# Second and third level of the expert mix on GpSimd: once for all five slabs of a group

## The reference, cut to what matters

```python
def _L0_ffn_ref(x, router_w, router_b, expert_w, expert_b):
    B, N, D, C, E, K = (8, 4096, 64, 64, 8, 2)
    router_probs = jax.nn.softmax(x @ router_w + router_b, axis=-1)
    top_p, top_i = jax.lax.top_k(router_probs, K)
    top_p = top_p / jnp.sum(top_p, axis=-1, keepdims=True)
    expert_out = jnp.einsum('bnd,edc->bnec', x, expert_w) + expert_b
    gathered = jnp.take_along_axis(expert_out, top_i[..., None], axis=2)
    return jnp.einsum('bnk,bnkc->bnc', top_p, gathered)
...
t = t + _L0_ffn_ref(_ln_t(t), L0_ffn_router_w, L0_ffn_router_b, L0_ffn_expert_w, L0_ffn_expert_b)
```

## Time and profile before

| | |
|---|---|
| median of 3 runs | 946.13 us |
| the profiled execution, its time | 946.58 us |
| its span in the profile | 944.4 us |
| granted TensorE clock, mean of the span | 0.977 |
| busy: TensorE, VectorE, ScalarE, GpSimd | 84%, 81%, 52%, 70% |
| L448, first level, 128x256 | 160 (slabs of prod) of 0.729 us |
| L453, second level, 128x128 | 200 of 0.457 us |
| L455, third level, 128x64 | 200 of 0.322 us |

### The profile page before, as it was taken

One profiled execution on the slowest core, in us unless ns is written; L12 is line 12 of the kernel. 1 busy time (PEld: TensorE's weight loads), 2 busy tenths in 40 slices (PEclk: granted clock), 3 DMA queues, 4 the chain that ended last, 5 costly groups with the idle time before them and its releaser, 6 DMA issues.

```text
span 944.4 us, 40376 instructions
## 1 busy us (share of the span) xinstructions
PE 791.5 (84%) x15174; PEld 500.7 (53%) x15174; DVE 767.1 (81%) x1810; ACT 488.1 (52%) x1061; POOL 664.0 (70%) x1092
## 2 busy tenths in 40 slices
PE   1444358999999999999999999999999999999743
PEld 1333125656665666666565656566656566666421
DVE  6776743688888888888988888888888888888754
ACT  3777213554555556554655465545554555555410
POOL 7899000367777777777776777677777777777777
PEclk9999999999999999999999999999999999999975
DMA  4554400001100110011001000111001100100000
GB/s 113 186 192 163 150 8 16 24 25 50 39 30 31 49 35 28 28 49 35 28 28 44 34 33 28 34 42 35 28 28 49 35 28 28 49 30 23 17 15 15
DMA packets 38088, 44.76 MB, mean 47 GB/s; under 512 B 6416, under 2 KB 32656, under 8 KB 38032
## 3 DMA queue, kind: packets, MB, share of 16 engines
q1 hardware_dynamic: 38032, 43.99, 14.2%
HBM read 14.48 MB, written 9.83 MB: 26 GB/s over the span
## 4 chain that ended last, share of the span: by engine, by line
DVE 34%; PE 34%; issue 20%; POOL 9%; ACT 1%; DVEq 1%; DMA 0%; POOLq 0%; SPq 0%; ACTq 0%
DVE negm L822 6%; PE psS L1090 6%; PE psS L1065 4%; DVE rinv L838 4%; POOL ln_s L398 4%; DVE prod L937 3%; PE ps_o L1147 3%; PE ps_x L1150 2%; PE ps_x L1147 2%; PE ps_o L1150 2%; DVE og L853 2%; DVE rt L899 2%; DVE q_lo L762 2%; POOL xn L401 2%; DVE ogu L845 2%
## 5 line engine op out<-in xcount | busy, mean ns | idle before, releaser
L448 POOL TENSOR_TENSOR add<-prod 128x256 f32<-128x256 f32 x160 | 116.7, 729 | 101.1 <-DVE prod L937 101.1
L822 DVE TENSOR_REDUCE negm<-psS 128x12 f16<-128x1920 f32 x80 | 146.0, 1825 | 12.5 <-PE psS L1075 8.7
L499 ACT ACTIVATE hl<-xn 128x320 f16<-128x320 f32 (+1 forms) x60 | 33.5, 559 | 158.4 <-POOL xn L401 156.9
L398 POOL TENSOR_TENSOR ln_s<-ln_v,half 128x5 f32<-128x5 f32 (+1 forms) x60 | 97.0, 1617 | 4.7
L453 POOL TENSOR_TENSOR add<-add 128x128 f32<-128x128 f32 x200 | 91.4, 457 | 0.1
L430 POOL TENSOR_TENSOR rinv_lo<-rinv,rinv_hi 128x160 f16<-128x160 f32 x40 | 19.7, 493 | 92.0 <-ACT rinv_hi L573 92.0
L542 ACT ACTIVATE pt_b<-psS 128x1920 f32<-128x1920 f32 x40 | 70.8, 1771 | 18.5 <-PE psS L1109 14.6
L1065 PE MATMUL psS<-bm,ident 128*128 128x480 f16 (+1 forms) x320 | 68.4, 336 | 9.2 <-issue 4.0
L494 ACT ACTIVATE sq<-xc 128x320 f32<-128x320 f32 (+1 forms) x60 | 33.4, 557 | 82.0 <-POOL xc L414 73.3
L455 POOL TENSOR_TENSOR ymix<-add 128x64 f32<-128x64 f32 x200 | 64.4, 322 | 15.7
L436 POOL TENSOR_TENSOR og_lo<-og,og_hi 128x320 f16<-128x320 f32 x80 | 61.7, 793 | 17.3 <-ACT og_hi L579 17.3
(11 more groups left out here) (263 smaller groups left out, 2819.9 us busy)
## 6 DMA issues: line engine op xcount, KB each, us to landing
xin<-in_x SPq DMA_DIRECT2D x20, 320.0 KB, 3.0
xs_all<-xs_pair SPq DMA_DIRECT2D x20, 320.0 KB, 2.5
xs_q<-xs_all SPq DMA_DIRECT2D x40, 160.0 KB, 2.1
xs_v<-xs_all SPq DMA_DIRECT2D x40, 160.0 KB, 2.1
xin<-in_x SPq DMA_DIRECT2D x40, 160.0 KB, 2.2
out<-res SPq DMA_DIRECT2D x40, 160.0 KB, 1.9
bias_scratch<-b_stage SPq DMA_DIRECT2D x20, 160.0 KB, 2.4
pt_a<-bias_scratch SPq DMA_DIRECT2D x1, 320.0 KB, 3.2
```

Source lines behind the costliest of these rows:

```text
L398: pool.tensor_tensor(ln_s[a][:, 3, 0:w], ln_v[a][:, 0:w], half[:, 0:w], ALU.pow).then_inc(own, 1)
L448: pool.tensor_tensor(add1[t % 2][:], prod_of(t)[:, 0:4, :], prod_of(t)[:, 4:8, :], ALU.add).then_inc(mix_step[t], 1)
L822: dve.tensor_reduce(negm[c][:, :, 0:slots], psS[:, :, 0:slots * N].rearrange("i h (s j) -> i h s j", s=slots), AX.X, ALU.max, negate=True) ...
```

## The change

`add1` and `add2` get a place for each of the five slabs (before: two buffers in turn). The first level stays as it is, slab by slab. The second level becomes one instruction over all five slabs (640 values a partition) and the third one more (320 values). Both are issued at the start of the next step of GpSimd, where the levels of slabs 3 and 4 were; the calls of `mix_rest` in the rest of the step go. `mix_step[t]` now counts first levels only, so its wait values change on GpSimd, ScalarE and DVE, and a new semaphore `mix_done` counts the two grouped levels.

```diff
--- before.py
+++ after.py
@@ -144,8 +144,8 @@
         prod = [sb(f"prod{a}", [P, 8, D]) for a in range(2)]
         kept = sb("kept", [P, 8, D])
         prod_of = lambda t: kept if t in KEPT else prod[WEIGHED.index(t) % 2]
-        add1 = [sb(f"add1{a}", [P, 4, D]) for a in range(2)]
-        add2 = [sb(f"add2{a}", [P, 2, D]) for a in range(2)]
+        add1 = sb("add1", [P, T, 4, D])
+        add2 = sb("add2", [P, T, 2, D])
         ymix = sb("ymix", [P, T, D])
         base = sb("base", [P, T, D])
         res = [sb(f"res{a}", [P, T, D]) for a in range(2)]
@@ -180,6 +180,7 @@
         ct_done, ct_evac, cb_done, base_done, res_done = sem("ct_done"), sem("ct_evac"), sem("cb_done"), sem("base_done"), sem("res_done")
         e_done, prod_done, mix_step, kept_done = [[sem(f"{name}{t}") for t in range(T)]
                                                   for name in ("e_done", "prod_done", "mix_step", "kept_done")]
+        mix_done = sem("mix_done")
         res_stored = [sem(f"res_stored{a}") for a in range(2)]
 
         x_flat = x.rearrange("a r j d -> (a r j d)")
@@ -445,26 +446,25 @@
             def mix_halves(g, t):
 
                 pool.wait_ge(prod_done[t], g + 1)
-                pool.tensor_tensor(add1[t % 2][:], prod_of(t)[:, 0:4, :], prod_of(t)[:, 4:8, :], ALU.add).then_inc(mix_step[t], 1)
-
-            def mix_rest(g, t):
-
-                pool.wait_ge(mix_step[t], 3 * g + 1)
-                pool.tensor_tensor(add2[t % 2][:], add1[t % 2][:, 0:2, :], add1[t % 2][:, 2:4, :], ALU.add).then_inc(mix_step[t], 1)
-                pool.wait_ge(mix_step[t], 3 * g + 2)
-                pool.tensor_tensor(ymix[:, t, :], add2[t % 2][:, 0, :], add2[t % 2][:, 1, :], ALU.add).then_inc(mix_step[t], 1)
+                pool.tensor_tensor(add1[:, t], prod_of(t)[:, 0:4, :], prod_of(t)[:, 4:8, :], ALU.add).then_inc(mix_step[t], 1)
+
+            def mix_rest(g):
+
+                for t in range(T):
+                    pool.wait_ge(mix_step[t], g + 1)
+                pool.tensor_tensor(add2[:], add1[:, :, 0:2, :], add1[:, :, 2:4, :], ALU.add).then_inc(mix_done, 1)
+                pool.wait_ge(mix_done, 2 * g + 1)
+                pool.tensor_tensor(ymix[:], add2[:, :, 0, :], add2[:, :, 1, :], ALU.add).then_inc(mix_done, 1)
 
             def residual(g, a):
 
-                for t in range(T):
-                    pool.wait_ge(mix_step[t], 3 * g + 3)
+                pool.wait_ge(mix_done, 2 * g + 2)
                 need(pool, res_done, g)
                 pool.tensor_tensor(base[:], ymix[:], x1[a][:], ALU.add).then_inc(base_done, 1)
 
             def step(n, a):
                 b = 1 - a
-                if on(n - 4): mix_rest(n - 4, 3)
-                if on(n - 4): mix_rest(n - 4, 4)
+                if on(n - 4): mix_rest(n - 4)
                 if on(n - 2): og_low(n - 2, 1)
                 if on(n - 2): og_low(n - 2, 0)
                 if on(n - 4): residual(n - 4, a)
@@ -475,11 +475,8 @@
                 if on(n - 2): norm2(n - 2, a)
                 if on(n - 3): mix_halves(n - 3, 1)
                 if on(n - 2): low2(n - 2, a)
-                if on(n - 3): mix_rest(n - 3, 1)
-                if on(n - 3): mix_rest(n - 3, 0)
                 if on(n - 3): mix_halves(n - 3, 2)
                 if on(n - 3): mix_halves(n - 3, 3)
-                if on(n - 3): mix_rest(n - 3, 2)
                 if on(n - 3): mix_halves(n - 3, 4)
 
             run_steps(pool, step)
@@ -609,7 +606,9 @@
             def keep_expert(g, t, bank):
 
                 act.wait_ge(e_done[t], g + 1)
-                need(act, mix_step[KEPT[KEPT.index(t) - 1]], 3 * (g - 1) + 1)
+                i = KEPT.index(t)
+                if i > 0: act.wait_ge(mix_step[KEPT[i - 1]], g + 1)
+                else: need(act, mix_step[KEPT[-1]], g)
                 act.activation(kept[:], bank[:].rearrange("p (e c) -> p e c", e=E), ACT.Copy, scale=1.0 / UP).then_inc(kept_done[t], 1)
 
             def keep_coef(g, bank16):
@@ -917,7 +916,7 @@
                 if k == 4: i = tt(rt[:, 0], rt[:, 7], rt[:, 2], ALU.add)
                 if k == 5:
                     for t in range(T):
-                        need(dve, mix_step[t], 3 * (g - 1) + 1)
+                        need(dve, mix_step[t], g)
                     i = tt(coef[:], rt[:, 0], wide(rs[:, 7, :]), ALU.mult)
                 if k == 6:
                     need(dve, ct_done, g)
@@ -932,8 +931,8 @@
                 dve.wait_ge(rt_tail, 7 * g + 5)
 
                 i = WEIGHED.index(t)
-                if i >= 2: dve.wait_ge(mix_step[WEIGHED[i - 2]], 3 * g + 1)
-                else: need(dve, mix_step[WEIGHED[i::2][-1]], 3 * (g - 1) + 1)
+                if i >= 2: dve.wait_ge(mix_step[WEIGHED[i - 2]], g + 1)
+                else: need(dve, mix_step[WEIGHED[i::2][-1]], g)
                 dve.scalar_tensor_tensor(out=prod_of(t)[:], in0=bank[:].rearrange("p (e c) -> p e c", e=E), scalar=1.0 / UP,
                                          in1=coef[:, t, :].unsqueeze(2).broadcast_to([P, E, D]),
                                          op0=ALU.mult, op1=ALU.mult).then_inc(prod_done[t], 1)
```

## The result

The changed kernel takes 991.46 us (median of 4 runs, 990.92 to 993.04) against 946.69 for the kernel before, a ratio of 1.043 (95% interval 1.035 to 1.051). The forecast was 994, in a range of 967 to 1003, slower.

A forecast was written before the change was run, and what follows sets the result against it. It took DVE's work ahead of the reciprocal L838, not GpSimd, to bound each step. 36 regular steps at +1.31 us gave +47.2, the rest +1: 946.13 + 48.2 = 994.3, so 994, range 967 to 1003.

The forecast's parts named there:

- The bound: GpSimd idles waiting for DVE's weighing L937; DVE's loss ahead of reciprocal L838 moves project_out and the whole 19.08 us step.
- GpSimd's time: Ten small adds, 3.90 us, become 128x640 at 1.54 and 128x320 at 0.86: 1.50 us less a group, no gain itself.
- rival D: The long GpSimd add is dearer, 2.29 us: about +1.5 a step, 1002; counted inside the main case's 0.70.
- First hold: DVE's coefficient half L926 starts inside slab 3's halves on GpSimd and is held until 527.14: +0.28 us.
- The routing: On DVE, L892, L893, L895 and L896 are held by the 128x320, both og_lo and base; L838 comes +1.31 us a step.
- the signs that were named: Expected in the new profile: step 20.4, L892 0.7 to 0.8, L899 0.20, GpSimd busy about 604, PE's wait over a us longer.
- The end: After the regular steps: three groups at 0 to +1 us each, last GpSimd burst about 1 us shorter; together +1.
- A (L926 slips through): L926 on DVE starts before slab 3's halves; L838 about +0.6 a step, 969; chance 0.14.
- B (a hold ends with a piece): GpSimd lets DVE through between an instruction's five pieces, no hold over 0.17 us; step stays 19.08, 945 to 946; chance 0.08.
- C (the saving counts): Where GpSimd ends the chain, 1.50 us a group come off; 943, or 886 over all 40 groups; chance 0.08.
- The prediction's rule: A DVE instruction with two SBUF operands, starting beside a running GpSimd instruction, is held to its end and about 0.06 us more.

The follow-up runs named there:

- base_after_routing: Changed kernel with one wait more: GpSimd begins base only when the routing's L899 on DVE is done; 985.0 us, ratio 1.042.
- pairs_in_block: Changed kernel with second and third levels still behind the last halves, but as ten slab-by-slab instructions instead of two; 979.75 us, ratio 1.037.
- merged_in_place: Order of the kernel before, upper levels merged for slabs 0, 1 and for slabs 3, 4, nothing moved; 988.9 us, ratio 1.049.
- no_upper_levels: Changed kernel with the two grouped adds left out, base being x1 + x1, so the result is wrong; 949.88 us, ratio 0.998.
- wait_placed_last: short_beside_routing with base's wait for L903 moved behind its other six waits; 936.73 us, ratio 0.990 against the kernel before.
- holds_alone: Separate kernel pairing one GpSimd instruction with small DVE instructions of several kinds to see which are held; its 50.55 us means nothing.
- short_beside_routing: Against the changed kernel: levels slab by slab, pairs of slabs 2 to 4 between the two og_lo, base after the routing; 942.86 us, ratio 0.995.
- two_merged: Against the changed kernel: only slabs 0 and 1 merged, behind slab 2's halves, og_lo ahead of pairs 3 and 4; 947.51 us, ratio 1.002.
- three_then_og: Against the changed kernel: slabs 0 to 2 merged behind slab 2's halves, og_lo ahead of small pairs 3 and 4; 1083.43 us, ratio 1.145.

## Why the prediction was right

**The bound.** That GpSimd has room and that what DVE loses ahead of the reciprocal moves the whole step was right: the reciprocal's lateness shows as PE's wait (50.5 us), and base_after_routing gives back 0.36 us a step for a hold of 0.35. The profiles bear it out more widely. DVE's small instructions (those that write lg, rt, rs, coef or c_stack) last 4.98 us together in a regular step of the kernel before. In the changed kernel, pairs_in_block, merged_in_place, base_after_routing and no_upper_levels they last 1.06, 0.89, 0.98, 0.70 and 0.21 us more, and the step is 0.96, 0.80, 0.87, 0.60 and 0.11 longer in the mean. Where a hold falls counts as well: in wait_placed_last they last 0.06 us more than before and the step is 0.24 shorter, its longest hold (L921) standing behind the reciprocal.

**GpSimd's time.** 1.54 and 0.86 were forecast, 1.550 and 0.879 measured; the saving of 1.5 us a step bought nothing, as said. Its 1.55 us also leave no room for rival D, the dearer add.

**First hold.** L925 at 0.72 as forecast, with L923 free at 0.19.

**The routing: a term mis-sized.** "L892 starts at 530.37" and is held by the 128x320: it was not. It starts 0.04 us ahead of the 128x320 (546.88 and 546.92), because the wait on five semaphores costs 0.17 us (545.11 to 545.28) and not the 0.07 of a pair. Had it cost 0.07, the 128x320 would have begun at 546.82, ahead of L891. Four instructions are held, but for 1.70 us in all and not 1.98. The step grew by 0.97 and not by 1.31 us; 36 x 1.31 = 47 should have been 36 x 0.97 = 35 (and only 35 intervals lie between the two rows that it counts from). So of the signs that were named, the step of 20.4 is 20.05, L892 of before reads 0.20 and not 0.7 to 0.8, L899 of before 0.55 and not 0.20, GpSimd is busy for 615.7 us and not 604, and PE's wait is longer by 0.92 us a step, not by more than one.

**What was missing.** The idle time of TensorE was seen, but not that its clock may drop behind it: 7.3 us in the profiled execution. The end cost 3.5 us where I took 1. These two made up for most of the mis-sized term, by luck; 994 is nearer to 991 than its working deserved.

**The rivals.** A (L926 slips through) did not come: the coefficient half is held in every step. B (a hold ends with a piece) is refuted by L892 of the timeline: it is held to 0.06 us after the end of the 128x320, which has five separate pieces; the add of holds_alone is in one piece and does not test this. C (the saving counts) is refuted for the regular steps by no_upper_levels, where all of the work is gone and the step is not shorter. The sentence of the Trainium skill, page Perfetto Trace Analysis, section Optimizing Scalar/DVE Operations, that grouping improves throughput of a saturated engine did not bear on this engine, which is busy for 70% of the span. The one on breaking instructions up fits short_beside_routing, which has ten adds in place of the two grouped ones and takes 48.6 us less than the changed kernel. The Trainium skill, page Advanced Engine Details and Errata, section GPSIMD Details, says that GpSimd conflicts with DVE instructions in a 2-port mode or with two SBUF inputs. That agrees with the kinds that holds_alone found held, if tensor_scalar and copy run in such a mode; the runs show only that they are held.

## What to carry to other kernels

Beside a chain of small SBUF-to-SBUF instructions on DVE, what counts on GpSimd is not its busy time but how long each of its instructions is, how many end while the chain runs, and where they stand. Merging them there saved GpSimd 1.5 us a step and cost the step 0.97; moving them there unmerged cost 0.81; merging two slabs away from the chain (two_merged) cost nothing that can be told. Put GpSimd's long instructions beside DVE's reductions and its instructions with an operand in PSUM (here the reciprocal), the short ones beside its small chains, and if need be let GpSimd wait, with that wait placed last. A DVE instruction that reads several times its shortest duration in the groups by form is the sign to look for.

## What was not expected of the hardware

The prediction's rule named two SBUF operands. One is enough for some kinds: tensor_scalar and copy on DVE are held beside a GpSimd add as long as those with two, 1.09 us, where a tensor_scalar without GpSimd beside it takes 0.17. This was expected by the time of holds_alone, as was that GpSimd's pow of 128x5 holds nothing. PE seems to have fetched its unchanged loop again in nearly every turn of three_then_og, 14 steps of 27.3 to 28.1 us, for a reordering on GpSimd alone. And TensorE's clock dropped in 5 of the 15 steps of the changed kernel in which it had been idle for 1.63 us, in none of those with 1.45 us, and in no regular step of the kernel before, where that idle time was 0.8 us at most.
